# One low part moved behind a row maximum, and query maxima ahead of a context collection, in a fused embedding, attention and ternary feed-forward kernel

## The reference, cut to what matters

```python
h = einsum("bnd,de->bne", patches(x), W_embed) + b_embed + pos_embed   # 64 images, 196 patches of 768
h = concatenate([h, txt], axis=1)                                     # 228 rows of 256 for each image
z = layernorm(h)
q, k, v = z @ Wq.T, z @ Wk.T, z @ Wv.T                                # 16 heads of 16
h = h + softmax(causal(q @ k.T / sqrt(16))) @ v @ Wo.T + bo
z = layernorm(h)
u = gelu(ternary(w_up) applied to z / rms(z))                         # 1024 wide, exact gelu
h = h + ternary(w_down) applied to u / rms(u)
```

## Time and profile before

| | |
|---|---|
| median of 3 runs | 1940.74 us (1939.0 to 1941.06) |
| profiled execution, its own time | 1944.63 us |
| its span, first to last instruction | 1942.6 us |
| busy: PE | 1855.9 us (96%) |
| busy: PEld | 1556.0 us (80%) |
| busy: DVE | 1571.8 us (81%) |
| busy: ACT | 1311.8 us (68%) |
| busy: POOL | 726.2 us (37%) |
| mean granted TensorE clock | 0.985 |

### The profile page before, as it was taken

One profiled execution on the slowest core, in us unless ns is written; L12 is line 12 of the kernel. 1 busy time (PEld: TensorE's weight loads), 2 busy tenths in 40 slices (PEclk: granted clock), 3 DMA queues, 4 the chain that ended last, 5 costly groups with the idle time before them and its releaser, 6 DMA issues.

```text
span 1942.6 us, 57163 instructions
## 1 busy us (share of the span) xinstructions
PE 1855.9 (96%) x24066; PEld 1556.0 (80%) x24066; DVE 1571.8 (81%) x2687; ACT 1311.8 (68%) x1920; POOL 726.2 (37%) x649
## 2 busy tenths in 40 slices
PE   5789999999999999999999999999999999999886
PEld 4668888888888888888888888888888888888765
DVE  4578888888888888888888888888888888888866
ACT  4447776677776676777676777667677667677654
POOL 1123333443433444333444343344433344433333
PEclk8899999999999999999999999999999999999988
DMA  4111122111112111112111111211111211111010
GB/s 142 27 47 30 52 57 57 52 38 36 51 52 57 52 44 42 40 52 57 52 54 39 33 52 56 57 52 38 37 50 52 57 52 50 38 38 40 31 35 25
DMA packets 66102, 93.54 MB, mean 48 GB/s; under 512 B 10082, under 2 KB 59718, under 8 KB 65592
## 3 DMA queue, kind: packets, MB, share of 16 engines
q1 hardware_dynamic: 65848, 89.90, 16.4%
HBM read 45.03 MB, written 14.94 MB: 31 GB/s over the span
## 4 chain that ended last, share of the span: by engine, by line
PE 66%; DVE 21%; ACT 7%; issue 5%; DMA 1%; POOL 1%; SPq 0%; POOLq 0%; ACTq 0%; DVEq 0%
PE dense L352 37%; PE score L352 18%; DVE gl L1029 7%; PE pvps L352 6%; DVE pT_lo L1005 4%; PE dense L409 3%; DVE rs L1015 2%; DVE mx L1057 2%; DVE qm L1071 2%; DVE mx L1059 2%; ACT sq L759 2%; ACT g L751 1%; PE dense L398 1%; ACT vp L784 1%; ACT pT_hi L718 1%
## 5 line engine op out<-in xcount | busy, mean ns | idle before, releaser
L1329 POOL TENSOR_SCALAR_AFFINE_SELECT pr<-pr 114x1368 f32<-114x1368 f32 x190 | 242.7, 1278 | 520.8 <-ACT pr L742 520.7
L742 ACT ACTIVATE pr<-score 114x1824 f32<-114x1824 f32 x190 | 320.8, 1689 | 59.6 <-PE score L352 59.3
L1029 DVE TENSOR_TENSOR gl<-g 128x456 f16<-128x456 f32 x256 | 229.8, 936 | 21.4 <-ACT g L751 20.7
L1341 POOL TENSOR_TENSOR acc<-acc,sq 128x456 f32<-128x456 f32 x190 | 237.4, 1250 | 22.8
L1057 DVE TENSOR_REDUCE mx<-score 114x4 f32<-114x912 f32 x192 | 211.6, 1102 | 30.7 <-PE score L352 30.7
L352 PE MATMUL dense<-wdn,g 128*114 128x256 bf16 x992 | 228.4, 278 | 1.5 <-ACT g L751 1.1
L352 PE MATMUL score<-qm,km 32*114 32x228 f32 (+1 forms) x4096 | 203.9, 324 | 21.3 <-DVE mx L1059 13.3
L352 PE MATMUL dense<-wdn,gl 128*114 128x256 bf16 x992 | 223.2, 273 | 0.0
L352 PEld LDWEIGHTS score<-qm,km 32*114 32x114 f32 x4096 | 157.8, 175 | 66.9 <-issue 57.5
L352 PE MATMUL score<-km,qm 32*114 32x228 f32 (+1 forms) x4096 | 202.6, 323 | 7.0 <-ACT pr L742 7.0
L1015 DVE RECIPROCAL rs<-rs 128x228 f32<-128x228 f32 x128 | 200.6, 1567 | 2.7 <-DMA cxraw<-cxraw 2.7
(11 more groups left out here) (145 smaller groups left out, 4541.5 us busy)
## 6 DMA issues: line engine op xcount, KB each, us to landing
pix<-x SPq DMA_DIRECT2D x32, 588.0 KB
sq<-x SPq DMA_DIRECT2D x32, 588.0 KB
rs<-cxraw SPq DMA_DIRECT2D x256, 57.0 KB, 2.0
cxraw<-cxraw SPq DMA_DIRECT2D x256, 57.0 KB, 2.0
out<-h SPq DMA_DIRECT2D x64, 228.0 KB
h<-txt SPq DMA_DIRECT2D x32, 64.0 KB, 4.6
km<-wqkvo SPq DMA_DIRECT2D x1, 1024.0 KB, 13.9
h<-w_upT SPq DMA_DIRECT2D x1, 1024.0 KB, 14.3
```

The lines of the kernel that those rows point to most:

```text
L742: act(probs(pair, q), score[0:R, :, 0:4 * R], ACT.Exp, scale=float(HD) ** -0.5).then_inc(a["exp"], 1)
L1029: tt(gl[:, m], g[:, m], hi_view(g[:, m]), ALU.subtract).then_inc(v["gl"], 1)
L1329: nc.gpsimd.affine_select(out=blocks, in_=blocks, compare_op=ALU.is_ge, fill=0.0, base=0, pattern=[[0, 4], [0, n], [1, R]], channel_multip ...
L1341: tt(acc[:], sq[:, 0] if m == 1 else acc[:], sq[:, m % 4], ALU.add).then_inc(p["acc"], 1)
```

## The change

In VectorE's step function two calls change their place. The low part of pixel group 4 is made after the second part of the row maxima of round 1, directly ahead of group 5, and no longer ahead of `scale_of` and of that maximum. In round 2 the maxima are added to the queries directly behind the eight `gelu_lo`, and `collect(t - 2, 1)` comes after them. No instruction is added or removed, and no other engine's order changes. The ending is as it was.

```diff
@@ VectorE, step(t, hs), in the loop over k
                         maxima_unit(t - 1, k, (0,))
                     if A and k == 1:
                         pixels_lo(t, 3)
-                        pixels_lo(t, 4)
                     if Dd and k == 1:
                         scale_of(t - 3)
                     if Dd and k == 2:
@@
                     if t == 2 and k == 0:
                         ternary(0, 1)
                     if A and k == 1:
+                        pixels_lo(t, 4)
                         pixels_lo(t, 5)
                     if Cc and k == 1:
                         collect(t - 2, 0)
                     if Dd and k == 2:
                         for m in range(8):
                             gelu_lo(t - 3, m)
+                    if Bm and k == 2:
+                        maxima_in_queries(t - 1, 1 - u, 0)
                     if Cc and k == 2:
                         collect(t - 2, 1)
-                    if Bm and k == 2:
-                        maxima_in_queries(t - 1, 1 - u, 0)
```

## The result

The changed kernel takes 1923.17 us (1921.95 to 1925.21, 4 runs) against 1940.9 us (1939.0 to 1941.25, 4 runs): ratio 0.9917, 95% interval 0.9905 to 0.9929, 17.7 us less. In a second measurement it is 1923.74 against 1940.57, ratio 0.991 (0.9897 to 0.9924). The forecast was 1921.8.

A forecast was written before the change was run, and what follows sets the result against it. TensorE's own work plus two stalls bound the kernel. Gains 0.24 + 0.46 less 0.05 make 0.65 us a step, times 29 is 18.9: from 1940.74 to 1921.8 us; likeliest range 1920 to 1925, 0.8 range 1918.5 to 1933.

The forecast's parts named there:

- stall 2: Round 2 into 3: TensorE's L398 transposes wait for the maxima added to the queries (L1071); removal gains 0.46 us a step.
- Stall 1: Round 1: TensorE's score matmuls wait for VectorE's second row maximum (L1059); removal gains 0.24 us a step.
- just holds, loss 0 to 0.01: Round 2: VectorE's xT_lo, usable at 858.57 to 858.67, wanted by TensorE at 858.66; loss 0 to 0.01 us.
- earlier scale chain: Round 1: scale chain comes 0.54 us earlier, but ScalarE's normalization queues behind the last pixel group's copy; nothing counted.
- The multiply's new neighbour: Second collection's multiply on VectorE overlaps GpSimd's first accumulation: about 0.1 us later, bounds 0 to 1.3; up to 0.6 free.
- The joint behind it: Rounds 3 to 4: ct_lo precedes GpSimd's mask, accl follows; sums of squares wait for accl, loss 0 to 0.15, taken 0.05.
- Collision at ct_lo: Rival, round 3: GpSimd's rstd holds off ct_lo, then the mask follows; loss 0.40 a step, 1932 us, chance 0.13.
- late-multiply rival: Rival: GpSimd's four accumulations hold off the collection's multiply in turn; 2.6 us longer a step, 2016 us, chance 0.05.

The follow-up runs named there:

- the half alone: Only the low part of pixel group 4 moved, against the kernel before: period 57.37 us, median 1933.88 us, ratio 0.9963.
- six copies: Changed kernel plus six one-element-per-partition copies on VectorE between the wait for xT_hi and the first xT_lo: 1931.6 us, ratio 0.9946 to the kernel before.
- late scale chain: Changed kernel with the scale chain also moved behind the second maximum in round 1: period 57.45 us, 1936.97 us, ratio 0.9985 to the kernel before.
- accl first: Changed kernel with accl (low sums of squares) ahead of ct_lo (low context part) in round 3: 1921.02 and 1921.0 us, period 56.95.
- collection later still: Changed kernel with the second collection moved behind both maxima of round 3: period 58.66 us, 1974.53 us, ratio 1.0181 to the kernel before.
- two copies: Changed kernel plus two one-element-per-partition copies on VectorE ahead of the first xT_lo: 1923.15 us, ratio 0.9917 to the kernel before.

## Why the prediction was right

The time came out within 1.4 us of the forecast, in its own range, and by its mechanism: both waits vanished, nothing took their place but the small one that was named. The gain was 17.7 us for a forecast of 18.9, and the mis-sized stall 2 (0.05 a step, 1.5 us in 29) is the main part of the difference. Two sizes behind the small loss were off and nearly cancelled, as told below.

*Stall 1, 0.24 a step*: measured 0.25 in the timeline, 0.26 as the period of the half alone.

*Stall 2, 0.46*: mis-sized, 0.41. The prediction took the time of four transposes from the second four, which have 82 rows to move, and put it in for the first four, which have 114. In the unbroken group of eight the first four take 1.09 - 0.64 = 0.45 and not 0.40.

*xT_lo "just holds, loss 0 to 0.01"*: right in its result, but the slack left is 0.13 us and not nothing, and the tight place is another. The prediction looked at the matmul that reads the second xT_lo; with six copies it is the first up product that waits, for the first xT_lo. It also said that ScalarE does not get earlier here and counted nothing for the earlier scale chain. From the weighted values of round 1 to xT_lo it was 857.35 - 851.87 = 5.48 and is 732.88 - 727.47 = 5.41, so 0.07 of the slack came by a little earlier ScalarE. That the delays of ScalarE's queue reach xT_lo in full the late scale chain confirms (0.54 in, 0.54 there).

*The multiply's new neighbour, 0.47 instead of 0.43*: 0.40. The multiply came at 746.36, 1.04 after the first accumulation had begun, as forecast (1.05), and was not held. The prediction took 1.3 for one accumulation, which is the distance from one to the next; by itself one takes 1.16 and so ended 0.12 later. That is too little to cost anything: the operations of VectorE that were held off in these traces end 0.13 to 0.15 less than their own time behind the end of their neighbour (the accl above ends 755.49, the mask 755.01, and 0.48 is 0.14 less than accl's own 0.62). The multiply of the earlier trace rows is alike: it ended 0.24 behind the mask, 0.16 less than its own 0.40.

*The joint behind it, loss 0.05*: 0.05 in the timeline, and the version with accl first gives back 0.06. The mechanism was as described: ct_lo ahead of the mask, mask stretched, accl behind it. The size is in part luck, because two steps in it were off and worked against each other. The chain to rstd and the mask was to move "by 0.15 at most" while TensorE moves by 0.70: stall 1's 0.24, less what the multiply was to lose. As the multiply lost nothing, the chain moved by the whole of stall 1, and ct_lo came 0.87 behind the start of rstd and not 0.70. By itself that gives accl more time. But a later ct_lo holds the mask longer: the mask ends 755.01 - 752.23 = 2.78 behind the start of rstd, where the prediction's figures give 879.25 - 876.76 = 2.49 (its rstd 0.15 earlier, at 876.76), and accl ends later with it. The two errors nearly cancel: that 0.05, picked between 0 and 0.15, came out is no proof of the figures behind it.

*Rivals.* Collision at ct_lo: ct_lo took 0.63, its free time. In the changed kernel that decides nothing, because it started 0.15 before the end of rstd, where a held operation would get in as well. The kernel with accl first decides it: there ct_lo starts at 865.82, with 0.47 of rstd left (864.95 + 1.34 = 866.29), and takes its free 0.63. The rival is wrong. The late-multiply rival, slower than before, would have needed several accumulations in a row. The low parts of the feed-forward blocks meet them so, in the changed kernel (DVE, then POOL):

```profile
739.37 4.27 DVE L1029 TENSOR_TENSOR gl<-g 128x456 f16<-128x456 f32 x3 [0.28 <-ACT g L751]
...
740.28 2.87 POOL L1341 TENSOR_TENSOR acc<-acc,sq 128x456 f32<-128x456 f32 x2
```

The three take 4.27, 1.4 each where one alone takes 0.63 (738.46), and the accumulations 1.4 instead of 1.16. The two engines take turns: each waits for one instruction of the other and not for several. But a kernel slower than before lay closer than that rival said. With the multiply 2 us later it is 1.8% slower, by a chain over h, the next mask and aT_lo that the prediction had not named.

## What to carry to other kernels

Measure a stall of a pipelined engine by the distance between the starts of its groups in places with and without the wait, and take the free distance from groups of the same shape. When a wait is removed, ask which of the chains behind it moves along: chains that start behind the stall move with it and keep their distances, and only those that started ahead of it close up. Where operations of VectorE and GpSimd hold one another off, such distances matter twice, since a multiply that arrived 0.14 us after its neighbour paid 1.12 us for it; a short operation that is wanted soon belongs in an idle gap ahead of the neighbour.

## What the runs showed of the hardware that was not expected

A pow on GpSimd does not hold VectorE off as a mask or an accumulation does. With accl first ct_lo (two SBUF inputs) starts 0.47 before the end of the pow of rstd and takes its free 0.63. In the kernel with the collection later still accl starts with 0.95 of it left (timeline of POOL and of DVE):

```profile
888.67 1.33 POOL L1370 TENSOR_TENSOR rstd<-ve,exps 114x4 f32<-114x4 f32 x1 [3.70 <-DVE ve L1213]
...
889.05 0.63 DVE L1251 TENSOR_TENSOR accl<-acc 128x456 f16<-128x456 f32 x1
```

The other way round, an operation of VectorE that started 0.17 before the pow stretched it from 1.02 to 1.34. The Trainium skill (SBUF — State Buffer, § Who interferes with whom) has whoever issues first keep the shared pair for the whole instruction. By that rule ct_lo and accl would have waited for the end of the pow; behind masks and accumulations VectorE did wait, which agrees with the rule (0.91 to 1.84), behind the pow it did not.

The wait behind a mask or an accumulation is shorter than the record of the neighbour by 0.13 to 0.15 us, so that an overlap of 0.12 (the multiply in the changed kernel) cost nothing.

Even operations on 114 x 4 elements wait: nb, with two SBUF inputs, took 1.37 us behind a mask where it takes 0.15.

A weight load that waits 0.23 us in the profile need not cost its matmul anything: in the kernel with two copies the period stayed at 57.01.
